# A local attention stage: P is divided ahead of its transpose, v is the stationary operand of P V, and five small edits to VectorE's order

## The reference

```python
h = shift_token(x)                  # half of the channels from the token before
q, k, v = split(h @ wqkv)           # 8 heads of 64
q = l2norm(q) * qs;  k = l2norm(k) * ksc
q, k = rotary_xpos(q, k)
sim = 8 * q @ k.T                   # masked: i < j or i > j + 64
o = softmax(sim) @ v
x = x + o @ wo
h = layernorm(shift_token(x)) * lg + lb
...
x = x + (a * gelu(g)) @ w2 + b2
```

## Time and profile before

| | |
|---|---|
| median of 3 runs | 1612.04 us (1609.6 to 1612.83) |
| the profiled execution: its own time, its span | 1622.13 us, 1619.9 us |
| granted TensorE clock, mean | 0.973 |
| busy: PE, DVE, ACT, POOL | 90%, 76%, 69%, 56% |
| d of layer 0, of layer 1 | about 877 to 1181 us, 1248 to 1550 us of the span |

### The profile page before, as it was taken

The page is one execution under the profiler, slowest core; times in us unless marked ns, Lnnn a source line. Parts: engine busy times, 40 slices in busy tenths (PEclk is TensorE's granted clock), DMA queues, the critical chain, the costliest instruction groups (busy, mean ns, idle before and its releaser), DMA issues.

```text
span 1619.9 us, 37516 instructions
## 1 busy us (share of the span) xinstructions
PE 1460.8 (90%) x11740; PEld 1196.8 (74%) x11803; DVE 1229.3 (76%) x3032; ACT 1110.5 (69%) x2666; POOL 908.2 (56%) x789
## 2 busy tenths in 40 slices
PE   4899999999988998888887899999898899999988
PEld 3677777777766776666665788888776788888866
DVE  6888888888755556888886788888666787777765
ACT  4888778877754556777774787787723778778732
POOL 4667778777731113444433777777401777777500
PEclk9999999999998997999998999999999999999999
DMA  9800000000012321210000000000000000000000
GB/s 380 325 1 8 11 10 10 11 11 17 13 53 69 87 79 28 62 39 22 22 19 9 13 15 15 15 14 16 10 11 5 5 17 14 15 15 14 11 24 34
DMA packets 87336, 62.62 MB, mean 39 GB/s; under 512 B 52037, under 2 KB 72901, under 8 KB 86469
## 3 DMA queue, kind: packets, MB, share of 16 engines
q1 hardware_dynamic: 83141, 53.00, 10.5%
q0 software_dynamic: 4096, 8.40, 1.8%
HBM read 21.30 MB, written 30.41 MB: 32 GB/s over the span
## 4 chain that ended last, share of the span: by engine, by line
PE 53%; DVE 27%; ACT 9%; issue 6%; POOL 3%; DMA 1%; DVEq 0%; another core or an unknown queue 0%; SPq 0%; POOLq 0%; ACTq 0%
PE slot L1685 6%; PE slot L461 5%; PE slot L463 4%; PE slot L462 4%; PE slot L1668 4%; PE slot L1629 4%; PE slot L1703 3%; PE slot L1638 3%; ACT a_p L743 3%; DVE a_sum L861 3%; PE slot L1938 2%; POOL a_rq L1106 2%; DVE a_ssq L971 2%; PE slot L1679 2%; PE slot L1189 2%
## 5 line engine op out<-in xcount | busy, mean ns | idle before, releaser
L1045 POOL TENSOR_TENSOR rs<-mv,nhalf 128x1 f32 (+1 forms) x160 | 96.6, 604 | 240.2 <-DVE mv L1040 175.1
L1854 POOL TENSOR_TENSOR d_A<-d_A,d_B 128x1024 f32<-128x1024 f32 x64 | 150.8, 2356 | 134.0 <-DVE d_B L1792 133.8
L1858 POOL TENSOR_TENSOR d_r<-d_vv,nhalf 128x16 f32<-128x16 f32 x64 | 186.5, 2914 | 47.5 <-DVE d_vv L1814 46.9
L743 ACT ACTIVATE d_p<-slot,d_nm,d_r 128x128 f32<-128x128 f32 x512 | 185.6, 468 | 27.2 <-DVE d_nm L1805 27.2
L743 ACT ACTIVATE a_p<-slot,a_nm,a_rq 128x77 f32<-128x77 f32 x512 | 163.7, 432 | 56.5 <-DVE a_nm L768 56.5
L743 ACT ACTIVATE c_p<-slot,c_nm 128x77 f32<-128x77 f32 x512 | 116.9, 359 | 30.2 <-DVE c_nm L1477 30.2
L1685 PE MATMUL slot<-d_v,d_pT 128*128 128x65 f32 x1024 | 121.8, 272 | 1.7 <-ACT d_pT L1722 1.7
L1685 PEld LDWEIGHTS slot<-d_v,d_pT 128*128 128x128 f32 x1024 | 119.4, 192 | 2.4 <-ACT d_pT L1722 2.1
L750 POOL TENSOR_TENSOR a_p<-a_p,a_rc 128x616 f32<-128x616 f32 x64 | 80.0, 1250 | 71.5 <-DVE a_rc L863 70.9
L1773 DVE TENSOR_TENSOR d_A<-slot,T 128x1024 f32<-128x1024 f32 x64 | 78.3, 1224 | 45.6 <-PE slot L1629 45.5
L1801 DVE TENSOR_REDUCE slot<-slot 128x8 f32<-128x1024 f32 x64 | 78.9, 1233 | 28.1 <-PE slot L1668 25.5
(11 more groups left out here) (288 smaller groups left out, 4495.2 us busy)
## 6 DMA issues: line engine op xcount, KB each, us to landing
routed<-zero SPq DMA_DIRECT2D x2, 9216.0 KB, 48.6
b_x<-routed SPq DMA_DIRECT2D x80, 64.0 KB
answers<-b_y SPq DMA_DIRECT2D x40, 128.0 KB
X<-in_x SPq DMA_DIRECT2D x2, 1024.0 KB, 8.1
d_zx<-Z SPq DMA_DIRECT2D x64, 32.0 KB
H<-Z SPq DMA_DIRECT2D x64, 32.0 KB
out<-f_o SPq DMA_DIRECT2D x8, 256.0 KB, 2.0
d_zx<-Z SPq DMA_DIRECT2D x64, 31.8 KB
```

The costliest lines, as they stand in the source:

```text
L743: i = e.activation(t["p"][:, h, :], R[slot][:, k // nbank, nk * (k % nbank):nk * (k % nbank) + nk], ACT.Exp, bias=t["nm"][:, h:h + 1], sca ...
L1045: return e.tensor_tensor(rs[:, bass.ds(b, 1)], mv[:, bass.ds(b, 1), 1:2].rearrange("p a b -> p (a b)"), nhalf[:, 0:1], ALU.pow)
L1854: e.tensor_tensor(t["A"][:, p, :], t["A"][:, p, :], t["B"][:, p, :], ALU.add).then_inc(S("d_key"), 1)
L1858: e.tensor_tensor(t["r"][:, it.m(2, 4), :], t["vv"][:, p, :], nhalf[:, 0:16], ALU.pow).then_inc(S("d_key"), 1)
```

## The change

- P is normalized before it is turned. Each exponential gives its row sum too (`accum_out`, 8 a batch), DVE takes the reciprocal of 8 sums and multiplies P (128x1024, in SBUF) with it. This stands first in DVE's step and waits for the second half of the exponentials of the step before.
- v (128x64) is the stationary operand, P^T (128 columns) the moving one. The result is O^T, of two heads on 128 partitions, in one bank. The column of ones, the four transposes of O and the division of O go.
- Maxima, factors and exponentials are split in two halves of 4 heads; on ACT the copy of P^T stands between the halves.
- The orders of PE, ACT and DVE in a step are changed. Rotary B's two halves stand ahead of and behind the maxima, the statistics' first instruction ahead of the sums of squares, the others behind them.
- The comparison with 1e-24 and the row's layernorm are written with two tensor operands in place of scalar forms.

```diff
@@ da_tensor: order now qkT(4), zT(1), v(2), S(4), PT(5), wo(6), qk(1), PV(5)
-                    if it.seen(5):
-                        e.wait_ge(S("d_exp"), it.upto(5, B))
                     e.wait_ge(S("d_key"), count(b, 3, 3, base=B))
                     for c in range(8):
+                        if it.seen(5) and c % 4 == 0:
+                            e.wait_ge(S("d_exp"), nth(it.upto(5, B), c // 4 + 1, 2))
                         mm = e.transpose(R[2][:, c // 4, 128 * (c % 4):128 * (c % 4) + 128],
...
+                b = it.b(5)
+                if b is not None:
+                    if it.seen(6):
+                        e.wait_ge(S("d_oTe"), it.upto(6, B))
+                    e.wait_ge(S("d_div"), count(b, 2, 2, base=B))
+                    for c in range(8):
+                        mm = e.transpose(R[3][:, c // 4, 128 * (c % 4):128 * (c % 4) + 128], t["p"][:, it.m(5, 2), c, :], ident[:])
+                    mm.then_inc(S("d_PT"), 1)
...
-                    for c in range(4):
-                        mm = e.transpose(R[1][:, 1, 128 * c:128 * c + 128], t["on"][:, it.m(6, 2), 128 * c:128 * c + 128], ident[:])
-                    mm.then_inc(S("d_OT"), 1)
...
-                        mm = e.matmul(R[3][:, h // 4, 65 * (h % 4):65 * (h % 4) + 65], t["pT"][:, 4 * (h % 2) + h // 2, :],
-                                      t["v1"][:, it.m(5, 4), h, :], start=True, stop=True)
+                        mm = e.matmul(R[3][DL * (h % 2):DL * (h % 2) + DL, 0, 128 * (h // 2):128 * (h // 2) + 128],
+                                      t["v"][:, it.m(5, 4), h, :], t["pT"][:, 4 * (h % 2) + h // 2, :], start=True, stop=True)
@@ da_scalar: order now qT(4), oT(6), v(2), high part(1), then
+                for half in range(2):
+                    b = it.b(4)
+                    if b is not None:
+                        r = t["r"][:, it.m(4, 4), :]
+                        e.wait_ge(S("d_max"), count(b, 2 * half + 2, 4, base=B))
+                        for j in range(4):
+                            k, h = 4 * half + j, 2 * j + half
+                            ex = e.activation(t["p"][:, it.m(4, 2), k, :], R[2][:, half, 128 * j:128 * j + 128], ACT.Exp,
+                                              bias=t["nm"][:, k:k + 1], scale=r[:, h:h + 1], accum_out=t["sum"][:, k:k + 1])
+                        ex.then_inc(S("d_exp"), 1)
+                    b = it.b(5)
+                    if b is not None and half == 0:
+                        e.wait_ge(S("d_PT"), count(b, base=B))
+                        e.activation(t["pT"][:].rearrange("p (a c) t -> p a (c t)", a=2), R[3][:], ACT.Copy).then_inc(S("d_pT"), 1)
@@ da_vector: order now P(5), A(2), row(0), B first half(2), low part(1), maxima and factors(4), B second half(2),
@@            statistics(7), squares(2), aggregate(7), add(6), comparison(2)
+                b = it.b(5)
+                if b is not None:
+                    e.wait_ge(S("d_exp"), count(b, 2, 2, base=B))
+                    e.reciprocal(t["rc"][:], t["sum"][:]).then_inc(S("d_div"), 1)
+                    e.wait_ge(S("d_div"), count(b, 1, 2, base=B))
+                    P = t["p"][:, it.m(5, 2), :, :]
+                    e.tensor_tensor(P, P, t["rc"][:].unsqueeze(2).to_broadcast([128, HL, 128]), ALU.mult).then_inc(S("d_div"), 1)
...
-                    e.tensor_scalar(rows(Z, b), rows(X, b), mv[:, bass.ds(b, 1), 0:1].rearrange("p a b -> p (a b)"),
-                                    rs[:, bass.ds(b, 1)], ALU.subtract, ALU.mult).then_inc(S("d_zn"), 1)
+                    e.scalar_tensor_tensor(out=rows(Z, b), in0=rows(X, b), scalar=mv[:, bass.ds(b, 1), 0:1].rearrange("p a b -> p (a b)"),
+                                           in1=rs[:, bass.ds(b, 1)].unsqueeze(2).to_broadcast([128, 1, D]),
+                                           op0=ALU.subtract, op1=ALU.mult).then_inc(S("d_zn"), 1)
...
+                    for k in range(2):
+                        top = R[1][:, 0, 4 * k:4 * k + 4]
+                        e.tensor_reduce(top, R[2][:, k, :].rearrange("p (j k) -> p j k", k=128), AX.X, ALU.max, negate=True)\
+                            .then_inc(S("d_max"), 1)
+                        e.wait_ge(S("d_max"), count(b, 2 * k + 1, 4, base=B))
+                        e.tensor_tensor(t["nm"][:, 4 * k:4 * k + 4], top,
+                                        t["r"][:, it.m(4, 4), 0:8].rearrange("p (j a) -> p a j", a=2)[:, k, :], ALU.mult)\
+                            .then_inc(S("d_max"), 1)
...
-                    e.tensor_scalar(t["vv"][:, p, :], t["ss"][:, p, :], 1e-24, None, ALU.max).then_inc(S("d_rot"), 1)
-                    e.reciprocal(rc, o[:, :, :, 64]).then_inc(S("d_div"), 1)
-                    e.tensor_tensor(t["on"][:, it.m(5, 2), :].rearrange("p (a j k) -> p a j k", a=2, j=4), o[:, :, :, 0:64],
-                                    rc.unsqueeze(3).to_broadcast([128, 2, 4, 64]), ALU.mult).then_inc(S("d_div"), 1)
+                    e.tensor_tensor(t["vv"][:, p, :], t["ss"][:, p, :], t["least"][:], ALU.max).then_inc(S("d_rot"), 1)
```

More of the change, by code:

```diff
@@ L300, in program @@
         d["qT"] = at("d_qT", [128, 8, 128])
-        d["on"] = at("d_on", [128, 2, 512])
+        d["sum"] = at("d_sum", [128, 8])
         d["oT"] = at("d_oT", [128, 4, 128])
@@ L310, in program @@
         d["vv"] = at("d_vv", [128, 2, 16])
+        d["least"] = at("d_least", [128, 16])
         d["r"] = at("d_r", [128, 4, 16])
-        d["v1"] = at("d_v1", [128, 4, HL, 65])
+        d["v"] = at("d_v", [128, 4, HL, DL])
         squares = room[0]
@@ L1631, in body @@
                     mm.then_inc(S("d_qkTp"), 1)
[L1632 to L1639, removed]
                 b = it.b(1)
@@ L1676, in body @@
                         e.wait_ge(S("d_hl"), it.upto(1, B))
-                    e.wait_ge(S("d_div"), count(b, 2, 2, base=B))
+                    e.wait_ge(S("d_oTe"), count(b, base=B))
                     for c in range(4):
-                        mm = e.transpose(R[1][:, 1, 128 * c:128 * c + 128], t["on"][:, it.m(6, 2), 128 * c:128 * c + 128], ident[:])
-                    mm.then_inc(S("d_OT"), 1)
[L1681 to L1684, removed]
-                        mm = e.matmul(R[3][:, h // 4, 65 * (h % 4):65 * (h % 4) + 65], t["pT"][:, 4 * (h % 2) + h // 2, :],
-                                      t["v1"][:, it.m(5, 4), h, :], start=True, stop=True)
-                    mm.then_inc(S("d_PV"), 1)
+                        mm = e.matmul(R[1][:, 1, 0:128], t["oT"][:, c, :], wol[:, l, c, :], start=(c == 0), stop=(c == 3))
+                    mm.then_inc(S("d_wo"), 1)
                 b = it.b(1)
@@ L1698, in body @@
                     mm.then_inc(S("d_qkp"), 1)
[L1699 removed]
+                b = it.b(5)
                 if b is not None:
[L1701 to L1704 removed]
+                    e.wait_ge(S("d_pT"), count(b, base=B))
+                    for h in range(HL):
+                        mm = e.matmul(R[3][DL * (h % 2):DL * (h % 2) + DL, 0, 128 * (h // 2):128 * (h // 2) + 128],
+                                      t["v"][:, it.m(5, 4), h, :], t["pT"][:, 4 * (h % 2) + h // 2, :], start=True, stop=True)
+                    mm.then_inc(S("d_PV"), 1)
             return body
@@ L1714, in body @@
                     e.activation(t["qT"][:].rearrange("p (a c) t -> p a (c t)", a=2), R[2][:], ACT.Copy).then_inc(S("d_qkT"), 1)
-                b = it.b(1)
+                b = it.b(6)
                 if b is not None:
[L1717 to L1722, removed]
+                    e.wait_ge(S("d_PV"), count(b, base=B))
+                    e.activation(t["oT"][:].rearrange("p c t -> p (c t)"), R[3][:, 0, :], ACT.Copy).then_inc(S("d_oTe"), 1)
                 b = it.b(2)
@@ L1829, in body @@
                     e.tensor_tensor(rows(Z, b), rows(Z, b), R[1][:, 1:2, 0:128], ALU.add).then_inc(S("d_add"), 1)
+                b = it.b(2)
+                if b is not None:
+                    e.wait_ge(S("d_rot"), count(b, 2, 3, base=B))
+                    if past(it.i - 4):
+                        e.wait_ge(S("d_key"), count(it.i - 4, 2, 3, base=B))
+                    if first_batch(it, 2) and l == 0:
+                        e.wait_ge(S("d_con"), 7)
+                    e.tensor_tensor(t["vv"][:, p, :], t["ss"][:, p, :], t["least"][:], ALU.max).then_inc(S("d_rot"), 1)
                 if it.static and it.i == NB:
```

79 lines of the change are left out of this document (35 added, 44 removed).

## The result

The changed kernel takes 1629.66 us (median of 5 runs, 1628.99 to 1635.11), the kernel before 1611.71 us on the same chip: ratio 1.0128, 95% interval 1.0113 to 1.0144, 1.3% slower. The forecast was 1638 us by the same mechanism. The profiled execution took 1629.66 us, with a span of 1627.6 us.

What follows compares the result with a forecast made beforehand. PE alone was taken to bound stage d at 8.85 us a step; a DVE-ACT loop with row sums would make it 9.32 and 9.26 us, 30 x 0.47 + 30 x 0.41 = 26 us: 1612 + 26 = 1638 us, range 1594 to 1682.

Steps and rivals of the forecast that it cites:

- DVE's part: Stage d, loop from reciprocal over P's product, A, row, half of B and low part to maxima and factors: 4.61 us.
- ACT's without sums: Stage d, eight exponentials, the copy of P^T between their halves and the hand-over, row sums not counted: 3.83 us.
- Both of the paths: Stage d, before sums: DVE's order in layer 0, 8.44 us; the copy of q^T in layer 1, 8.38 us.
- PE's own work: Stage d, PE's work a step falls by 1.1 us to 7.75 us, without O's transposes and with cheaper P V.
- The sums: Eight row sums on ACT in stage d's loop, 0.11 us each, 0.88 us in all, between 0 and 2.64.
- slack of 1.5 us: PE in stage d: products with wo and of q and k move past each other within this room.
- rival 1: Row sums free or nearly so: steps of 8.44 and 8.38 us, 1586 us, faster; chance 0.2.
- Rival 2's hold: DVE's L1040 held 0.85 us by POOL's A + B; rival 2: no change, 1609 to 1612 us, chance 0.1.
- Theory A: One-tensor-forms run with statistics early: only DVE's two-tensor form is held beside POOL, so the comparison takes 0.16 us again.
- Rival 4: Layer 0's row on DVE caught behind POOL's product with k, up to 1.04 us: 1653 to 1669 us; chance 0.13.
- Rival 3: Row sums wait for ACT's pipe, 0.2 to 0.33 us each: 1681 to 1744 us, much slower; chance 0.12.
- The ends of the layers: End of each layer's chain: loses 2.0 us, gets 2.4 us; set at 0, 2 us either way.

Runs made afterwards that it cites:

- P ahead and B ahead: Changed kernel with P's transposes ahead of the scores, P^T's copy ahead of all exponentials and B's second half ahead of the maxima: 1620.3 us, 8.84 us a step.
- P ahead: Changed kernel with P's transposes ahead of the scores, P^T's copy ahead of all exponentials, O^T's copy ahead of q^T's: 1650.4 us, 9.31 us a step.
- the run without sums and hold: Changed kernel without row sums (reciprocal of a constant one) and with the variance's addition as two one-tensor instructions: 1615.8 us, 8.92 us a step.

## Why the prediction was right, and where it was not

**The mechanism.** PE leaves the bound, and a loop from the reciprocal over DVE to the maxima and over ACT's exponentials and the copy of P^T back sets the step. This is shown by its waits, by four more transposes on PE that cost nothing, and from the side of its members: B in it costs 0.60 us a step and P^T's copy out of it (with B in) takes the step from 9.70 to 8.84. DVE's part was put at 4.61 us and is 1007.30 - 1002.78 = 4.52; ACT's without sums was put at 3.83 and is 4.58 - 0.74 = 3.84. Both of the paths were right: by DVE's order in layer 0, by the copy of q^T in layer 1. PE's own work was put too low: P V takes 11.35 - 10.32 = 1.03 us, as forecast, but with waits of only 0.38 and 0.48 us PE is busy for 8.25 us of a step and not 7.75.

**The sums, a term mis-sized.** Eight at 0.11 us were 0.88; the next exponential starts 0.092 us after a read on average, 0.74 for eight. With this value the two sums of the forecast give 8.44 + 0.74 = 9.18 and 8.38 + 0.74 = 9.12, against 9.11 measured. The estimate from the Trainium skill (ScalarE: Activation LUTs, What ACT_TABLE_LOAD costs), 94 ns a sum, is nearer than the value I took, and the rows agree with it at 92 ns. That its +19 us for the kernel stand so near to the +18 measured is luck: the steady steps alone make 60 x 0.26 = 15.6 us, the ends of the layers, which both sums had at nothing, add 6.2, and 4 go the other way for a reason that stays open. Two small slips: by its own bounds of 0.07 to 0.15 us a sum the forecast goes from 1619 us and not from 1623, and the halving costs 0.23 us by its terms and not 0.25. Nothing turns on either.

**The step that failed: what other products have as room.** "PE's products with wo and of q and k move past each other within its slack of 1.5 us", and B's second half was costed at nothing, since what follows the factors on DVE was said to "have until 9.3". I asked how long B could wait for POOL and not that PE's product of q and k waits for it, with P V and the transposes of q and k behind. That makes a loop of 8.92 us, only 0.19 under the one that I forecast. So rival 1 had a wrong price: with the sums taken out altogether the kernel takes 1615.6 us and not 1586, still 0.5% slower than before. A chance of 0.2 for faster rested on a term by which this order could not have become faster. The sign was safe for a reason that I did not see, and to that extent it is luck.

**Rival 2's hold** came as described: L1041 takes 0.95 us and ends with POOL's sum. It costs nothing here, since DVE waits 0.44 us for the exponentials behind it, and nothing without the sums either, since the loop over B stands above it. The Trainium skill (SBUF - State Buffer, Who interferes with whom) names two kinds of VectorE instruction that contend with GpSimd: those with two inputs in SBUF, and one-tensor forms that run in a 2-port mode. Beside POOL's sum the traces agree: 128x2 with two inputs took 0.95 us, 128x16 in the one-tensor form 1.15, and 128x1 in the one-tensor form 0.15 (no row shows in which mode each ran). Theory A, that no one-tensor form is held, had left the second kind out. Beside POOL's power the rule is too wide: P's product has two inputs in SBUF and starts 0.50 us behind that power, at 1003.01, well within its 2.91 us, and takes 1.22 us all the same.

**Rival 4** did not come: the row takes 0.34 us at +2.51 of the step, ahead of POOL's product with k. It lies beside POOL's power, which ends at +2.64, and is not held by it. Rival 3 did not come: the exponentials start 0.44 us apart.

**The ends of the layers** I had set at 0 ± 2 us. They cost more. The last product A of layer 0 and the first of layer 1, before:

```profile
1146.80 1.22 DVE L1773 TENSOR_TENSOR d_A<-slot,T 128x1024 f32<-128x1024 f32 x1
...
1246.20 1.22 DVE L1773 TENSOR_TENSOR d_A<-slot,T 128x1024 f32<-128x1024 f32 x1
```

and after:

```profile
1141.22 1.22 DVE L1782 TENSOR_TENSOR d_A<-slot,T 128x1024 f32<-128x1024 f32 x1
...
1244.00 1.22 DVE L1782 TENSOR_TENSOR d_A<-slot,T 128x1024 f32<-128x1024 f32 x1
```

99.4 us became 102.8, and from the last A of layer 1 to the end 103.7 became 106.5: 6.2 us for both. With P ahead and B ahead the two are 105.0 and 109.5, 11.4 us above before, and this is why a step as short as before did not bring back the time. Which of the moved pieces costs it was not tried. The steps and the ends together make 22 us; the medians differ by 18. The remaining 4 us stay open. The profiled execution of before reached d 14 us later than that of after. Of these, 8 are there at the start of stage c already, which the change does not touch: its first product with the head masks starts at 610.4 us before and at 602.0 after. Some 10 may belong to that one execution of before, which was 10 us above its median.

No version tried beats the kernel before. Four loops, over PE's own work (8.85 in the order of before), over the exponentials (9.11), over B (8.92) and, with P ahead, from P's transposes to the scores (8.8 to 8.9), lie within 0.3 us of each other, so taking time out of one alone is worth at most the distance to the next.

## What to carry to other kernels

When an engine at 99% is relieved, list every wait between engines of the new order and add up each closed loop through them, those with an "off-path" piece behind another engine's wait too: a gain ends at the second longest loop, and that sets the price of the rivals as well. A row sum on ACT is an instruction, not free; in a loop it counts at the distance of starts. Removing a visible hold is worth nothing until the loop it lies in is shown to be the longest; take it away alone and look at the step.

## What the runs showed of the hardware that was not expected

- The read of the accumulator is shown at 0.19 to 0.24 us (mean 0.213) but moves the next exponential by only 0.092 us, for 128x128 exponentials.
- Scores with 64 rows a head take 1.16 us for 8 heads when heads on the two halves of the array's rows alternate, 1.71 when four of one half come in a row.
- POOL's power of 128x16, 2.91 us, takes 3.97 when DVE's product of two tensors starts 0.03 us ahead of it (the run without sums): the hold works in both directions. Here it was off every loop. It goes with who starts first: in the run without sums and hold the power starts 0.05 us ahead of the product, and neither is held, 2.91 and 1.25 us. The run with P ahead has both cases, 3.97 us and 2.91, as the product starts 0.03 us ahead of the power or 0.07 behind it. The timelines of DVE and of POOL in the run without sums:

```profile
1002.81 1.23 DVE L1776 TENSOR_TENSOR d_p<-d_p,d_rc 128x1024 f32<-128x1024 f32 x1
```

```profile
1002.84 3.97 POOL L1874 TENSOR_TENSOR d_r<-d_vv,nhalf 128x16 f32<-128x16 f32 x1 [0.48 <-DVE d_vv L1844]
```

And the two in the run without sums and hold:

```profile
1002.34 1.25 DVE L1781 TENSOR_TENSOR d_p<-d_p,d_rc 128x1024 f32<-128x1024 f32 x1
```

```profile
1002.29 2.91 POOL L1879 TENSOR_TENSOR d_r<-d_vv,nhalf 128x16 f32<-128x16 f32 x1 [0.21 <-DVE d_vv L1849]
```
